# A two-layer graph kernel: gathers begun before the pass count is known, set-up reordered, column numbers loaded a round at a time

## What is computed

```python
# layer 0                                    # layer 1
h = relu(edge_feat @ W1 + b1)                h = relu(dist[:, None] @ w1 + b1)
w = (h @ W2 + b2).reshape(e, 4, 8, 8)        R = h @ w2 + b2            # 64*7 paths, with 3x3 frames
m = paths(x[src], edge_sh, w)                m = paths(x[src], harmonics(rel_vec), R)
out = segment_sum(m, dst) + x @ si           out = segment_sum(m, dst)
x = layernorm(x + out)                       x = layernorm(x + out)
```

## Time and profile before

| | |
|---|---|
| median of 3 runs | 4053.04 us |
| the profiled execution's own time | 4059.36 us |
| its span | 4057.4 us |
| PE busy | 3377.3 us (83%) |
| DVE busy | 3460.9 us (85%) |
| POOL busy | 2953.0 us (73%) |
| ACT busy | 2184.8 us (54%) |

### The profile page before, as it was taken

One profiled execution on the slowest core, in us unless ns is written; L12 is line 12 of the kernel. 1 busy time (PEld: TensorE's weight loads), 2 busy tenths in 40 slices (PEclk: granted clock), 3 DMA queues, 4 the chain that ended last, 5 costly groups with the idle time before them and its releaser, 6 DMA issues. The chain is left out here.

```text
span 4057.4 us, 95500 instructions
## 1 busy us (share of the span) xinstructions
PE 3377.3 (83%) x23156; PEld 1945.7 (48%) x23156; DVE 3460.9 (85%) x5277; ACT 2184.8 (54%) x6587; POOL 2953.0 (73%) x3087
## 2 busy tenths in 40 slices
PE   4777777777777777777559999999999999999996
PEld 3444444444444444444335555555555555555553
DVE  8888888888888888888759999889889888988887
ACT  3555555555555555555335565555555555555554
POOL 5777777777777777777377777777777777777772
PEclk7888888888888888888779999999999999999998
DMA  3111111111111111111212222222221222222221
GB/s 107 35 33 32 34 32 33 34 33 35 32 33 32 33 32 34 36 32 33 35 38 48 45 44 44 44 44 44 47 45 41 47 44 44 44 43 44 44 44 28
DMA packets 238827, 162.68 MB, mean 40 GB/s; under 512 B 143937, under 2 KB 212594, under 8 KB 238066
## 3 DMA queue, kind: packets, MB, share of 16 engines
q1 hardware_dynamic: 104338, 91.78, 8.7%
q0 software_dynamic: 98560, 50.66, 8.6%
q10 hardware_dynamic: 35650, 17.88, 1.7%
HBM read 148.83 MB, written 10.43 MB: 39 GB/s over the span
## 5 line engine op out<-in xcount | busy, mean ns | idle before, releaser
L430 POOL DMA_INDIRECT rows<-x_rows,src x1540 | 1483.2, 963 | 536.6 <-issue 526.6
L430 POOL DMA_INDIRECT rows<-in_x,src x1540 | 1468.9, 954 | 485.6 <-issue 472.3
L775 PE MATMUL red<-prod,ident 128*128 128x336 f32 (+1 forms) x4704 | 1511.2, 475 | 1.4 <-DVE prod L1073 1.2
L775 PEld LDWEIGHTS red<-prod,ident 128*128 128x128 f32 x4704 | 892.3, 195 | 635.4 <-issue 193.3
L1073 DVE TENSOR_TENSOR prod<-wps,arena 128x896 f32<-128x896 f32 x782 | 832.4, 1083 | 176.2 <-PE wps L762 159.0
L755 PE MATMUL wps<-bias_parts,ones 64*128 64x448 bf16 (+1 forms) x2346 | 471.4, 398 | 610.7 <-DVE prod L1067 452.4
L565 ACT ACTIVATE gap<-iota,slot_plan 128x128 bf16<-128x128 f32 x3136 | 935.6, 386 | 7.0
L762 PE MATMUL wps<-w_sb,hidden 64*128 64x448 f32 (+1 forms) x3920 | 746.9, 476 | 0.0
L583 ACT ACTIVATE arena<-red 128x336 f32<-128x336 f32 (+1 forms) x294 | 135.5, 461 | 1103.5 <-PE red L775 1102.9
L755 PEld LDWEIGHTS wps<-bias_parts,ones 64*128 64x128 bf16 x2346 | 114.6, 94 | 1135.3 <-DVE prod L1067 562.4
L1082 DVE TENSOR_REDUCE arena<-prod 128x384 f32<-128x3072 f32 (+1 forms) x195 | 520.9, 2671 | 0.1
(11 more groups left out here) (127 smaller groups left out, 3025.3 us busy)
## 6 DMA issues: line engine op xcount, KB each, us to landing
mlp<-in_dist SPq DMA_DIRECT2D x196, 256.0 KB
fetched<-in_x SPq DMA_DIRECT2D x3072, 0.1 KB
fetched<-x_rows SPq DMA_DIRECT2D x3072, 0.1 KB
mlp<-in_feat SPq DMA_DIRECT2D x98, 256.0 KB
rows<-in_x,src POOLq DMA_INDIRECT x1540
rows<-x_rows,src POOLq DMA_INDIRECT x1540
frames<-frame ACTq DMA_DIRECT2D x49, 144.0 KB
geo<-frames ACTq DMA_DIRECT2D x98, 72.0 KB
```

The source lines that it names most:

```text
L430: nc.gpsimd.indirect_dma_start(out=rows[z][:, t, :], out_offset=None, in_=table_rows, in_offset=bass.IndirectOffsetOnAxis(ap=src_sb[z][:, ...
L775: ins = nc.tensor.matmul(red[:, bank * 512:bank * 512 + cols], ident[:], pr[:, i, :, a:b, :], start=(i == 0), stop=(i == MUL - 1))
```

## The change

It has these parts.

1. **First pass with the count unknown.** POOL and SP no longer read the pass count ahead of layer 0. They enter the loop at once and read it into a register at the end of each pass (`read_passes`). The first pass always takes place.
2. **Set-up.** SP issues only the load of the targets by rows, then goes straight to its stream. ACT issues the other loads, in the order weights, self term, table, `rel`, `dst`, layer 1 weights. PE sets the semaphores' first values. The iotas come from HBM with the identity, and the maximum over partitions is made by a PE product with the identity and a DVE reduction. Scatter keys take three DVE operations in place of eight. ACT squares the lengths between the store and the reload of the window numbers.
3. **Column numbers.** DVE loads the eight column numbers of a round in one register load at the round's start, in place of four at each body's start. In the last round one load of twelve takes the place of three of four. The last whole round stands behind the loop, written out.
4. **Last frames between the layers.** The frames of the last round are made after the normalization of layer 0 and stored then. The scaling of the layer 1 weights (`prepare_second`) follows them, still before the loop of layer 1.
5. **Last chunk of layer 1.** Its tiles 8 to 11 are summed by DVE (`sum_tiles`) and no longer by PE: the second PE sum covers two tiles in place of six.

```diff
@@ SP, POOL
+        def read_passes(eng, register):
+            eng.wait_ge(windows_known, 1)
+            eng.reg_load(register, passes_i[0:1, 0:1])
...
             sp.dma_start(dst_i[0:N_GROUPS // 4, :], dst_rows).then_inc(loaded["dst_rows"], 16)
-            sp.dma_start(w1_sb[:], w1_0).then_inc(loaded["weights"], 16)
...
-            sp.dma_start(rel_sb[:], rel).then_inc(loaded["rel"], 16)
...
+                    if n == 0:
+                        read_passes(sp, count)
-            count = passes(sp)
-            stream(0, count)
+            stream(0, sp.alloc_register("sp_passes"))
+            count = passes(sp)
...
-            pool.wait_ge(spans_reduced, 1)
-            nc.gpsimd.partition_all_reduce(span_max[:, 1:2], span_max[:, 0:1], P,
-                                           bass.bass_isa.ReduceOp.max).then_inc(spans_known, 1)
...
+                    if n == 0:
+                        read_passes(pool, count)
-            count = passes(pool)
-            gather_all(0, count)
+            gather_all(0, pool.alloc_register("pool_passes"))
+            count = passes(pool)
@@ ACT
+            act.dma_start(w1_sb[:], w1_0).then_inc(loaded["weights"], 16)
...
+            act.dma_start(table[:, 0:BLOCKS, :], x_nodes).then_inc(loaded["nodes"], 16)
+            act.dma_start(rel_sb[:], rel).then_inc(loaded["rel"], 16)
+            act.dma_start(dst_t[:], dst).then_inc(loaded["dst"], 16)
...
+            spread_windows()
             square_lengths()
-            spread_windows()
+            read_windows()
             root_lengths()
...
             deviations(0)
-            act.wait_ge(frames_stored, act.snap(count * (16 * ROUNDS) + 16))
+            act.wait_ge(loaded["l1_weights"], 48)
+            store_frames(ROUNDS - 1, act.snap(count * FRAME_ROUNDS + 1))
+            act.wait_ge(frames_stored, act.snap(count * (16 * FRAME_ROUNDS) + 32))
@@ PE
+            pe.wait_ge(loaded["weights"], 64)
+            pe.wait_ge(spans_reduced, 1)
+            nc.tensor.matmul(hps[:, 0:P], span_max[:, 0:1].broadcast_to([P, P]), ident, start=True, stop=True
+                             ).then_inc(spans_known, 1)
...
-                        weigh(n, z1, r1, range(5, halves))
-                        sum_products(n, z1, r1, 1)
+                        weigh(n, z1, r1, range(5, halves), last=last)
+                        sum_products(n, z1, r1, 1, last)
@@ DVE
+            chain(nc.vector.tensor_reduce(span_max[:, 1:2], hps[:, 0:P], AX_X, ALU.max))
...
-            chain(nc.vector.tensor_copy(target, dst_t[:]))
-            chain(nc.vector.tensor_single_scalar(dst_t[:], dst_t[:], P - 1, ALU.bitwise_and))
...
-            chain(nc.vector.tensor_tensor(negkey0, negkey0, by_chunk(rest_), ALU.add))
+            st.done(nc.vector.tensor_scalar(negkey0, by_chunk(dst_t[:]), 0.0, FAR, ALU.is_lt, ALU.mult))
+            chain(nc.vector.tensor_tensor(low, dst_t[:], low_bits[:].broadcast_to([P, CHUNKS * TILES]), ALU.bitwise_and))
+            st.done(nc.vector.tensor_tensor(negkey0, negkey0, by_chunk(low), ALU.subtract))
+            measure()
...
-            def load_columns(k):
+            def load_columns(k, chunks):
...
-                if z == 0:
-                    make_frames(i, r, Steps(dve, frame_steps, (r - 1) * FRAME_STEPS))
+                if z == 0 and not last:
+                    make_frames(i, frames_of)
...
+                elif not tail:
+                    sum_tiles(1, z1, r1, st, last)
                 add_window(3, cols, z1, st)
...
-                    with dve.Fori(0, ROUNDS - 1) as i:
+                    def whole_round(i):
                         r = round_of(dve, j, i)
+                        cols = load_columns(i * RING, RING)
                         for z in range(RING):
...
-                            body(n, i, z, r, st, False, False, load_columns(i * RING + z))
+                            body(n, i, z, r, st, False, False, cols[z],
+                                 dve.snap(j * FRAME_ROUNDS + (i + 1)))
+                    with dve.Fori(0, ROUNDS - 2) as i:
+                        whole_round(i)
+                    whole_round(ROUNDS - 2)
...
-                    cols = [load_columns(k) for k in range(CHUNKS - RING, CHUNKS + 1)]
+                    cols = load_columns(CHUNKS - RING, RING + 1)
...
             normalize(0)
             first_windows()
+            make_frames(ROUNDS - 1, dve.snap(count * FRAME_ROUNDS + 1))
+            prepare_second()
             dve.wait_ge(x1_stored, len(PIECES) * 16)
```

More of the change, by code:

```diff
@@ L599, in loop, with body @@
                 s = layers[n]
-                def body(i, z, r, last, steps):
+                def body(i, z, r, last, steps, frames_of=None):
                     k = i * RING + z
@@ L609, in body @@
                         distances(n, z1, r1, 0, steps)
-                    if n == 0 and z == 1:
-                        store_frames(i, r)
+                    if n == 0 and z == 1 and not last:
+                        store_frames(i, frames_of)
                     if not last:
@@ L714, in _ @@
         def _(pe):
+            for s in layers:
+                for semaphore, count in s.per_chunk:
+                    pe.sem_inc(semaphore, count)
+                pe.sem_inc(s.tile_moved, 16)
+            pe.sem_inc(frames_stored, 16)
+            pe.wait_ge(loaded["weights"], 64)
+            pe.wait_ge(spans_reduced, 1)
+            nc.tensor.matmul(hps[:, 0:P], span_max[:, 0:1].broadcast_to([P, P]), ident, start=True, stop=True
+                             ).then_inc(spans_known, 1)
             pe.wait_ge(loaded["self"], 32)
@@ L734, in sum_hidden, with weigh @@
                                  ).then_inc(s.hidden_summed[z], 1)
-            def weigh(n, z, r, halves, first=False):
+            def weigh(n, z, r, halves, first=False, last=False):
                 s = layers[n]
@@ L1149, in add_window, with body0 @@
                 add_window.last = st.done(nc.vector.tensor_tensor(window, window, split[z][:, g, :], ALU.add))
-            def load_columns(k):
+            def load_columns(k, chunks):
                 _, cols = nc.values_load_multi_w_load_instructions(
-                    offs[0:1, bass.ds(k * GROUPS, GROUPS)], engines=(mybir.EngineType.DVE,), min_val=0,
+                    offs[0:1, bass.ds(k * GROUPS, chunks * GROUPS)], engines=(mybir.EngineType.DVE,), min_val=0,
                     max_val=(BLOCKS - 1) * FEAT)
-                return cols
-            def body0(i, z, r, st, last, tail, cols):
+                return [cols[c * GROUPS:(c + 1) * GROUPS] for c in range(chunks)]
+            def body0(i, z, r, st, last, tail, cols, frames_of):
                 s = layers[0]
@@ L1196, in body0 @@
                 if not tail:
-                    sum_tiles(0, z1, r1, st, LAST_TILES if last else TILES)
+                    sum_tiles(0, z1, r1, st, last)
                 add_window(2, cols, z1, st)
@@ L1276, in prologue1, with body @@
                 sum_tiles(1, 0, r, st)
-            def body(n, i, z, r, st, last, tail, cols):
-                (body0, body1)[n](i, z, r, st, last, tail, cols)
+            def body(n, i, z, r, st, last, tail, cols, frames_of=None):
+                (body0, body1)[n](i, z, r, st, last, tail, cols, frames_of)
             def loop(n, count):
```

141 lines of the change are left out of this document (64 added, 77 removed).

## The result

The changed kernel takes 4094.6 us (median of 4 runs, 4090.97 to 4096.94), the kernel before 4051.7 us beside it: a ratio of 1.0106, 95% interval 1.0090 to 1.0122. It is slower by 43 us, where 14 were predicted. Direction and mechanism were right, the size was not, and the time lies above the range.

A forecast was written before the change was run, and what follows sets the result against it. POOL's gathers were taken to bound the kernel, in layer 1 by only 1.0 us a round. Terms -17 - 3.4 - 2.8 + 31 + 6 = +14 us on the median 4053 gave 4067 us, range 4041 to 4086.

The forecast's parts named there:

- The gathers' start: Start of layer 0: first gather at 8.0 us instead of 26.35, gaining 17 us, bounds 9 to 20.
- the thin cover: Set-up: DVE reaches `project_sum` of chunks 0 and 1 before POOL needs it, with 2 us to spare at the closer place.
- The 2.22 us gather: Set-up before the change: a gather beside the scatter keys took 2.22 us instead of 0.95, agreeing with two-port exclusion.
- Between the layers: Last round of layer 0 to layer 1: moved frames and joined loads gain 3.4 us, bounds 2 to 6.
- The end: End of layer 1: load of twelve and smaller second PE sum gain 2.8 us, bounds 1 to 5.
- The load's delay: First bodies in layer 1: load of eight adds 1.4 us a round, losing 31 us, bounds 17 and 59.
- The clock: Layer 1: PE's waits bring half-clock stretches in 4 of 47 rounds, losing 6 us, bounds 0 and 30.
- The bound of 30 us: Upper bound on the loss from clock drops in layer 1, forecast at 6 us.
- From the profiled run to the median: Whole kernel: profiled run lay 6.3 us above the median; the +14 us was applied to the median, 4053 to 4067.
- A: Rival, layer 1: load of eight takes what four take, clock stays, parts cancel: 4053 us; chance 0.26.
- C: Rival, set-up: early start gives nothing, all the loss in layer 1 stays: 4084 us; chance 0.09.
- B: Rival, layer 1: delay partly made up within the round, under 1.0 us, gathers still bind: 4030 us; chance 0.15.

The follow-up runs named there:

- light kernels: Kernels with SP's single-row fetching replaced by one transfer of 32 fixed rows: 4050.1 us for the kernel before, 4093.6 us for the changed kernel.
- four and four: Changed kernel with four column numbers loaded at each body: 4028.9 us with SP's single-row fetching left out, 4042.2 us with it in place.
- six and two: Changed kernel, SP's single-row fetching left out, first body loading six column numbers, second body two: 4049.9 us, ratio 0.9977.
- seven and one: Changed kernel, SP's single-row fetching left out, first body loading seven column numbers, second body one: 4097.1 us, ratio 1.0095.

## Why the prediction was right in kind and wrong in size

**The gathers' start** was put at 8.0 us and was 8.56. The third and fourth chunk of gathers waited for nothing, so the thin cover held: DVE was at `project_sum` of chunks 0 and 1 at 44.73 and 69.72, where 49 and 71 were forecast. Of the 17.8 us there were 13.5 left at the end of layer 0. POOL's busy time there is 1472.6 us against 1468.9: some gathers take longer. The first 64 of them account for 0.7 us; the others are spread over the layer. Whether the load of eight has a part in this is open. Among the light kernels it was 1942.1 us from first to last gather with four and four and 1951.4 with eight, on one chip. But with the single rows in place it was 1949.6 us with four and four and 1949.4 with eight and no check, as much as the 1948.6 of the changed kernel, where the kernel before took 1944.2. The 2.22 us gather, which the prediction names for VectorE's two-port modes, ran beside a `TENSOR_TENSOR` for most of its time, as the 2.83 us one did after: it shows that work of DVE can hold a gather up, not that a two-port mode did.

**Between the layers** 4.3 us came off in the gathers' times (3.4 predicted), and 1.6 of them were lost again before the first body of layer 1. **The end** gave 3.7 us for 2.8: DVE idles 2.31 and 1.66 us there for 3.21 and 2.45, and the 4.35 us are gone.

**The load's delay** had the mechanism right and the size too small: 1.57 us in a round in place of 1.4. That the whole of a delay comes into the round held too, also for the 0.97 us of six and two. The values (1.1) and the load (0.26 for the 0.3) were as worked out; the 0.22 us by which the load begins later was in no row of before. 47 x 0.17 = 8 us.

**The clock** is the step whose reasoning failed. I counted drops by the share of long waits that had brought one before, 2 in 13, and took 4 of 47 rounds at 1.6 us. There were 14 at 0.91: 12.7 us for 6.4, so 6.3 us more. The old waits came now and then. The new one stands in every round, and the drops then come on a beat, 122.9 us apart (every third round) for most of the 14; nothing in the earlier trace rows told that. The price of 1.6 us was that of a drop 1.7 us behind the end of PE's wait (2723.2 to 2724.9 before), and the new ones stand right at its end. So too few drops, each too dear, gave a product that by luck missed less than its count did. The bound of 30 us did hold.

Together: 8 + 6.3 in layer 1, 3.5 in layer 0, 0.7 between, 0.9 less at the end is 17.6 us, and the profiled run's own sum was missed by 18 (31.8 measured, 13.8 predicted).

**From the profiled run to the median** another 11 us went: the medians are 42.9 apart, the profiled runs 31.8. I noted that the profiled run of before lay above its median, and still moved the difference over unchanged. The profiled run of before (4059.4) was slower than all four that its median is taken from, that of after (4091.0) the fastest of its four; before's time hangs on the gathers in both layers, after's in one. The bounds of the range had nothing for this, and it is the largest single miss: without these 11 us the time would have been 4083.5 us, inside the range. The layer 1 terms that were too small (+31 and +6 forecast, +51.7 measured) and this step put the time outside together; neither would have done it alone.

**The rivals.** A (cheap load, no drops) and C (no gain at the start) were wrong. B was wrong for this kernel, and its point of decision too: it was put at 1.0 us a round, and is 0.65. With four and four 4028.9 us were measured and without the check 4029.9, near B's 4030, but not for B's reason: four and four have no delay, and without the check `sum_tiles` covers the load. Nothing is made up within the round.

**The Trainium skill**, "Runtime: NRT & Kernel Launch", section "Instruction fetch mechanics", gives about 200 ns for each register of a load. By it eight would take 0.8 us more than four; the trace has 0.26. But six took 0.81 and seven 1.05 us in all, so each value beyond four costs about 0.24 there, near the figure of the Trainium skill. The trace disagrees with it for four and eight, and comes near it for the values beyond four in six and seven.

## What to carry to other kernels

Where one engine's register work stands in front of the instruction that another engine waits for, count the values and their checks, not the loads: joining two loads of four saved one load of 0.34 us, which was hidden, and put 1.6 us where nothing hid them. And where two chains race, the delay that is free is the difference of their whole times over all rounds (here 30 us over 47 rounds), not the difference of their paces in the steady state. If the checks can go, they are the first thing to take out.

## What the runs showed of the hardware

- A load of registers on DVE takes 0.34 us for four values, 0.60 for eight and 0.85 for twelve, but 0.81 for six and 1.05 for seven. The load of seven alone takes longer than that of eight; with the checks of the values the delay of a first body is 1.48 us for seven and 1.57 for eight.
- A checked value costs 0.275 us of register instructions behind the load; unchecked it costs none that the trace shows.
- PE's pause of 1.36 us in each round brought 14 stretches at half clock in layer 1, and 1.38 us of products without use in its place brought none and made the kernel 13 us faster in that layer.
- A stretch of 3.4 us at half clock cost 0.91 us where it began within 0.3 us of the end of PE's wait (changed kernel) and about 1.6 us where it began 1.5 to 1.8 us behind it (seven and one, and the kernel before).
- The long gathers of the set-up ran beside DVE work of several forms, among them a `TENSOR_TENSOR` of 2.29 us with both operands in SBUF (a gather of 2.83 us in place of 0.94); beside the `TENSOR_REDUCE` of 2.29 us behind it gathers took 0.94.
